# Stage orders of two attention layers, and logit indices loaded once: a four-layer graph network on one Trainium2 core

## The reference

```python
z = leaky_relu(xl[src] + xr[dst] + ee, 0.2)          # first and third attention layer
score = einsum('ehc,hc->eh', z, att)
m = segment_max(score, dst)
a = exp(score - m[dst])
denom = segment_sum(a, dst)
out = segment_sum(xl[src] * a / denom[dst], dst)
...
e = leaky_relu(h[src] @ a_src + h[dst] @ a_dst, 0.2)  # layer 2: edge logits
...
msg = all_msgs[edge_src, rel]                         # layer 3: 16 relation matrices
out = segment_sum(msg, edge_dst)
```

## Time and profile before

| | value |
|---|---|
| median of 3 runs | 7174.21 us |
| lowest, highest | 7170.84, 7176.18 us |
| profiled execution: its time | 7206.94 us |
| its span, first to last instruction | 7205.2 us |
| mean granted TensorE clock | 0.71 of full speed |
| DVE busy, share of the span | 75% |
| POOL busy, share of the span | 66% |
| PE busy, share of the span | 54% |
| ACT busy, share of the span | 44% |
| stage a, first to last gather start | 657.0 to 1724.7 us |
| stage g, first to last gather start | 5488.2 to 6528.8 us |
| logit stage, first to last gather start | 3456.2 to 3985.2 us |

### The profile page before, as it was taken

One profiled execution on the slowest core, in us unless ns is written; L12 is line 12 of the kernel. 1 busy time (PEld: TensorE's weight loads), 2 busy tenths in 40 slices (PEclk: granted clock), 3 DMA queues, 4 the chain that ended last, 5 costly groups with the idle time before them and its releaser, 6 DMA issues. The chain is left out here.

```text
span 7205.2 us, 84156 instructions
## 1 busy us (share of the span) xinstructions
PE 3879.4 (54%) x13024; PEld 2314.5 (32%) x13024; DVE 5386.3 (75%) x16939; ACT 3173.0 (44%) x7568; POOL 4760.7 (66%) x4609
## 2 busy tenths in 40 slices
PE   0001667664666665899000689868886766772000
PEld 0000233332333333788000345763332433441000
DVE  4502888886777777888676899767887888887886
ACT  0001666664333333777444100224554666665555
POOL 1777777775777776776677556016664777774776
PEclk9999776776788887555555789558997676665555
DMA  6001555555433343111799100569994555554554
GB/s 191 4 1 29 97 99 97 99 96 79 90 85 84 85 85 72 47 47 45 112 120 115 25 7 8 158 144 131 154 153 101 115 114 115 115 114 114 165 169 137
DMA packets 915728, 687.80 MB, mean 95 GB/s; under 512 B 604705, under 2 KB 754495, under 8 KB 914973
## 3 DMA queue, kind: packets, MB, share of 16 engines
q1 hardware_dynamic: 517456, 403.54, 21.1%
q0 software_dynamic: 147200, 139.08, 19.9%
q10 hardware_dynamic: 250888, 143.42, 6.6%
HBM read 491.36 MB, written 227.64 MB: 100 GB/s over the span
## 5 line engine op out<-in xcount | busy, mean ns | idle before, releaser
L802 POOL DMA_INDIRECT b_xg<-t_H,c_at x784 | 833.2, 1063 | 284.0 <-issue 238.4
L802 POOL DMA_INDIRECT g_xg<-t_D,c_at x784 | 803.4, 1025 | 320.1 <-issue 238.2
L802 POOL DMA_INDIRECT a_xg<-t_XL,c_at x784 | 830.6, 1059 | 250.3 <-issue 238.8
L1822 POOL DMA_INDIRECT f_dg<-t_D,c_at x392 | 377.0, 962 | 555.9 <-POOLq L179 358.7
L2210 POOL DMA_INDIRECT out<-n_yo,c_at x392 | 430.9, 1099 | 235.1 <-issue 116.1
L440 POOL DMA_INDIRECT t_XL<-su_pos,su_scatx x392 | 389.8, 994 | 245.6 <-DMA t_XL<-in_nodes 126.4
L1326 POOL DMA_INDIRECT l_d<-t_D,l_ix x392 | 397.7, 1014 | 183.8 <-issue 121.4
L1141 POOL DMA_INDIRECT t_RANK<-m_place,m_at x392 | 397.9, 1015 | 163.2 <-issue 116.4
L938 ACT ACTIVATE a_hn<-a_xg,a_sm 128x64 f32<-128x64 f32 x784 | 269.8, 430 | 401.0 <-DVE a_sm L675 400.1
L1375 ACT ACTIVATE l_hn<-l_xs,l_sm 128x64 f32<-128x64 f32 x784 | 265.0, 426 | 295.6 <-DVE l_sm L675 211.9
L2189 ACT ACTIVATE n_h<-n_x,n_sm 128x64 f32<-128x64 f32 (+1 forms) x800 | 269.4, 426 | 210.0 <-DVE n_sm L675 210.0
(11 more groups left out here) (455 smaller groups left out, 14037.6 us busy)
## 6 DMA issues: line engine op xcount, KB each, us to landing
a_ends<-t_LAST SPq DMA_DIRECT2D x98, 256.0 KB, 5.1
t_XSD<-a_xg SPq DMA_DIRECT2D x98, 256.0 KB
t_H<-a_oE ACTq DMA_DIRECT2D x98, 256.0 KB
b_ends<-t_LAST SPq DMA_DIRECT2D x98, 256.0 KB
l_xb<-t_XSD SPq DMA_DIRECT2D x49, 512.0 KB
f_rl<-t_REL SPq DMA_DIRECT2D x49, 512.0 KB
g_xb<-t_XSD SPq DMA_DIRECT2D x98, 256.0 KB
g_ends<-t_LAST SPq DMA_DIRECT2D x98, 256.0 KB, 5.2
```

The lines of the kernel that those rows point to most:

```text
L802: nc.gpsimd.indirect_dma_start(xg[k][:, j, i, :], None, table, bass.IndirectOffsetOnAxis(ap=C["at"][:, i, n * J + j:n * J + j + 1], axis=0 ...
L1822: nc.gpsimd.indirect_dma_start(dg[k][:, u, j, :], None, T["D2"], bass.IndirectOffsetOnAxis(ap=C["at"][:, 0, (2 * n + u) * J + j:(2 * n + u ...
```

## The change

Three edits. In stage a, DVE meets `denominator` first instead of behind `quotients`, and `quotients` go behind `sums`; ACT meets `normed` ahead of `features`; PE's `results` move from the end of the step to a place between `project` and `scores`, one step later (lag 5 instead of 4). In stage g, DVE's `norm` goes from the end of the step to its head with the same lag 1, ACT's `normed` gets lag 1 instead of 2, ACT's `results` lag 6 instead of 5, PE's `project` lag 2 instead of 3, `moments` lag 7 instead of 6, and PE's order in a step is new. In the logit stage the 49 index loads are replaced by one load of all indices into a tile `C["source"]` that outlives the blocks, issued by SP at the end of `mlp_block`; with them go SP's wait for landed gathers and POOL's wait for `ix`, and POOL's loop is written out in full. Stage b (wide) keeps its orders.

```diff
             if wide:
                 stages = [(L, leaky), (L + 2, quotients), (L + 1, denominator), (L + 1, sums), (L, maximum)]
+            elif tag == "a":
+                stages = [(4, denominator), (3, leaky), (4, sums), (5, quotients), (3, maximum), (1, norm)]
             else:
-                stages = [(L, leaky), (L + 2, quotients), (L + 1, sums), (L, maximum), (L - 2, norm)]
-                if not both:
-                    stages.insert(2, (L + 1, denominator))
+                stages = [(1, norm), (3, leaky), (5, quotients), (4, sums), (3, maximum)]
             flow(dve, stages, slots=SL)
...
+            elif tag == "a":
+                stages = [(3, values), (2, normed), (3, features), (2, turned), (3, exponents), (5, results)]
             else:
-                stages = [(L, values), (L, features), (L - 1, normed), (L - 1, turned), (L, exponents), (L + 2, results)]
+                stages = [(3, values), (3, features), (2, turned), (1, normed), (3, exponents), (6, results)]
             flow(act, stages, slots=SL, looped=tag != "a")
...
+            elif tag == "a":
+                stages = [(3, project), (5, results), (3, scores), (2, turn)]
             else:
-                stages = [(L, project), (L, scores), (L - 1, turn), (L + 1, results)]
-            if tag == "g":
-                stages.append((L + 3, moments))
+                stages = [(2, turn), (7, moments), (3, scores), (2, project), (4, results)]
             flow(pe, stages, slots=SL)
...
             flow(sp, [(0, load)], slots=SL)
+            sp.dma_start(C["source"][:, :].rearrange("p (n j) -> p n j", j=LOGIT_ROWS),
+                         T["PSRC"].rearrange("(n p j) -> p n j", p=P, j=LOGIT_ROWS)).then_inc(s_source, 16)
+            sp.wait_ge(s_source, 16)
...
                 if old:
-                    sp.wait_ge(s_g[k], NG * q)
-                sp.dma_start(ix[k][:, :], words_by(T["PSRC"], n, K)).then_inc(s_ix[k], 16)
-                if old:
-                    sp.wait_ge(s_xs, n - SL + 1)
+                    hold(sp, s_spturn, (s_xs, n - SL + 1))
...
             def gather(n, k, q, old):
-                hold(pool, s_turn, (s_ix[k], 16 * (q + 1)))
                 if old:
                     hold(pool, s_turn, (s_xs, n - SL + 1))
                 for j in range(K):
                     nc.gpsimd.indirect_dma_start(
                         d1[k][:, 0, j, :], None, T["D1"],
-                        bass.IndirectOffsetOnAxis(ap=ix[k][:, j:j + 1], axis=0)).then_inc(s_g[k], 16)
-            flow(pool, [(0, gather)], total=NB, slots=SL)
+                        bass.IndirectOffsetOnAxis(ap=C["source"][:, n * K + j:n * K + j + 1], axis=0)).then_inc(s_g[k], 16)
+            flow(pool, [(0, gather)], total=NB, slots=SL, looped=False)
```

More of the change, by code:

```diff
@@ L1121, in mlp_block @@
         s_at, s_rank, s_rturn, s_spturn = m.sems("at", SL), m.sems("rank", SL), m.sem("rturn"), m.sem("spturn")
+        s_source = m.sem("source")
         rank = T["RANK"].unsqueeze(1)
@@ L1278, in _ @@
                 act.wait_ge(s_st[k], 16 * chunks_of(k, SL))
+LOGIT_ROWS = 8
 def logit_block(nc, T, C):
@@ L1288, in logit_block @@
         SL = 4
-        K = 8
+        K = LOGIT_ROWS
         NB = EP // (P * K)
         slots = range(SL)
-        ix = [m.sb(f"ix{k}", [P, K], I32) for k in slots]
         d1 = [m.sb(f"d1{k}", [P, 2, K, D]) for k in slots]
@@ L1300, in logit_block @@
         sm = m.sb("sm", [P, 6, 2 * K])
-        s_ix, s_g, s_ld, s_hs, s_es = (m.sems(x, SL) for x in "ix g ld hs es".split())
-        s_xs, s_f, s_hn, s_e, s_ch, s_che, s_turn = (m.sem(x) for x in "xs f hn e ch che turn".split())
+        s_g, s_ld, s_hs, s_es = (m.sems(x, SL) for x in "g ld hs es".split())
+        s_xs, s_f, s_hn, s_e, s_ch, s_che, s_turn, s_spturn = (m.sem(x) for x in "xs f hn e ch che turn spturn".split())
         block = ctx.enter_context(nc.Block())
@@ L2267, in program @@
         C["at"] = m.sb("at", [P, 2, EF], I32)
+        C["source"] = m.sb("source", [P, EF], I32)
         prologue_block(nc, a, T, C)
```

## The result

The changed kernel takes 7089.07 us, median of 3 runs (7082.77 to 7089.41). Its ratio to the kernel before is 0.9871, 95% interval [0.9857, 0.9884], and 85 us less by the medians, whose own quotient is 0.9881.

A forecast was written before the change was run, and what follows sets the result against it. POOL's gathers, stretched by DVE scans on two SBUF tiles, were taken to bound stages a and g, DMA transfers the logit stage. Stage a -18, stage g 0, its end +8, logit -5 gave -15 us: median 7174.2 to 7159, range 7124 to 7189.

The forecast's parts named there:

- The bound: Stages a and g: POOL's gathers set the pace; their stretch, 88 and 61 us, is all a new order can win.
- phases are tied to landings while DVE waits, and DVE will wait in most steps: Stage a: reason for taking 18 us less, the stretch going from 0.90 to 0.72 us a step.
- a triangle's mean of 0.4: Stage a, rival of freely drifting scans: `den` stretches gathers 0.4 us a step on average, 49 us less; total 7128; chance 0.22.
- DVE's floor with 61 us: Stage a: largest gain allowed, if DVE's own work bounds the step at 10.3 us instead of 10.92: 61 us less.
- PE's and ACT's edits in stage a at nothing: Stage a: the moved PE and ACT work costs nothing, hidden by POOL's pace.
- I take 0: Stage g: no change in the gathers' stretch, since 58 of 98 steps already run without leaky's wait and the mean is 0.62.
- The ends (31 more, 61 less): Stage g: bounds around 0; 31 us more if each `num` catches a gather by 0.94, 61 less if none does.
- The end of stage g, +8: After stage g's last gathers: three rounds instead of two follow, a round taking 8.4 us, so 8 us more.
- The logit stage, -5: Logit stage: 5 us less, 3 for the start and 2 for the 49 little loads; ends 0 and -14.
- the 3 us of the start: Logit stage: the 3.05 us from SP's first issue to the first gather go almost whole, 3 us less.
- the 2 us of the little loads: Logit stage: dropping the 49 little loads gains 2 us of the 10.8 us that POOL waits for `ix` inside.
- the 18 us given to stage a: Stage a: stretch of 0.72 instead of 0.90 us a step over 98 steps, 18 us less; bounds 0 and 61 less.

The follow-up runs named there:

- before_msg_psum: Kernel before, all lists old, with stage a's product written to a PSUM bank as an operand of `num`: 7126.63 us, ratio 0.9945.
- after_more_dve: Changed kernel with a DVE memset of 290 columns (0.300 us) ahead of stage a's running maximum: 7108.23 us, ratio 0.9901 to the kernel before.
- a_only: Kernel before with the three new lists of stage a alone: 7112.99 us, ratio 0.9913.
- a_dve_only: Kernel before with DVE's new list of stage a alone, PE and ACT keeping their old orders there: 7123.87 us, ratio 0.992.
- g_moments_as_before: Changed kernel with stage g's `moments` last in PE's list again, at lag 6: 7086.73 us, ratio 0.9874 to the kernel before.
- g_shift: Kernel before with a DVE memset of 290 columns (about 0.3 us) ahead of stage g's product: 7149.39 us, ratio 0.9957.
- logit_only: Kernel before with the edit of the logit stage alone: 7160.7 us, ratio 0.9988.
- before_again: Kernel before with no edit, run once more for a second profiled execution: 7174.79 us, ratio 1.0004.
- b_msg_psum: Changed kernel with stage b's product written to the eighth PSUM bank: 7059.81 us, ratio 0.9841 to the kernel before.

## Why the prediction was wrong

**The bound, right.** POOL's gathers, stretched by DVE, were what could be won: the whole gain of stages a and g is in their busy time, and before_msg_psum shows the mechanism without any change of order. The Trainium skill, page "SBUF — State Buffer", section "Who interferes with whom", says that a VectorE instruction with two SBUF inputs contends with a GpSimd instruction that reads SBUF; the PSUM operand that freed the gathers agrees. What the section reports of a probe, that `tensor_tensor` did not stall the generation of descriptors, does not hold here: the product, a `tensor_tensor`, held the gather of 5691.50 by 0.35 us.

**Stage a: the step that failed is "phases are tied to landings while DVE waits, and DVE will wait in most steps".** Its first half was right: `num` goes off the gathers, `den` takes 0.72 where DVE waits, as in the early steps (10.7 us each). But it was worked out for a DVE that waits and then never asked whether the new pace leaves it anything to wait for. The same text had the floor, 10.2 to 10.5 us, beside a forecast step of 10.02 + 0.72 = 10.74; that looks like 0.3 us of room. But the room depends on the stretch. All ten waits for a landing lie in the first ten steps, the last six of them 0.31 to 0.41 us long. Then DVE halts 0.31 us (764.08) and 0.25 us (774.52) as its loop begins, `den` meets the next gather later and stretches it by 0.22 instead of 0.75, and POOL's step shrinks with it to 10.02 + 0.22 = 10.24, beside DVE's own 10.22: nothing is left to wait for.

From there DVE's pace, 10.29 with the loop's turns, is above POOL's undisturbed 10.02, and `den` slides to where it stretches the gathers by just the difference: 10.29 - 10.02 = 0.27 a step, measured 0.29. I took a triangle's mean of 0.4 for this case and called it a rival, with 0.22. The end named for it, DVE's floor with 61 us, is what came (55 to 59). That DVE is nearly the bound there now was tried (after_more_dve). What frees the phase was not tried and stays open. Six other traces with this DVE list, a_only and a_dve_only among them, show the same halts and a pace of 10.29 to 10.30; but in one of them, g_moments_as_before, DVE's last wait for a landing came at 687 us already, before any halt.

**PE's and ACT's edits in stage a at nothing: right** (a_dve_only).

**Stage g: the step that failed is "I take 0".** The reason for it, that 58 of 98 steps ran without leaky's wait already, took the time from the add to `num` as all that counts. That is not so: after the change that time is 5.96 and 6.47 us in two neighbouring steps. It also left out the product and the add, which held gathers for 10 and 12 us before. What changed is where the add itself begins, 0.3 to 0.5 us behind a gather's start, where before it was near it or 1.2 behind. `num`'s share of the stretch fell from 39 to 4 us, the whole from 58 to 23. The ends (31 more, 61 less) held the measured -35 to -38, but the middle was chosen by counting steps of the old pattern. g_shift shows that the scan's place against the gathers moves the time by itself; the moments' place and the late loads are excluded. Why the rows land at the other lag, 1.9 instead of 1.6 us behind the last gather's end, stays open: with the old lists one of seven profiled executions (logit_only) ran that way too.

**The end of stage g, +8: right**, 49.6 instead of 42.9 to 45.5, so 4 to 7.

**The logit stage, -5: the 3 us of the start measured 2.4; the 2 us of the little loads are 0** within what profiles tell. The 10.8 us of waits that this term was taken from were nearly all the first profile's own: inside the stage POOL waits for index loads 1.2 us in a_only and never in before_again.

**The sum.** -18 + 0 + 8 - 5 was forecast. Against before_again it is -55 in stage a, -35 in g, +4 at its end, -3 at the logit head: -89 by the stages. The spans of these two profiled executions differ by 77.5 us only, since in this pair the rest took some 10 us longer: stage b by 3, the logit stage by 2, the blocks between it and stage g by 7. The medians say 85, the ratio 92 us. So the direction and the cause came out as forecast, and the size did not: the 18 us given to stage a belong to a phase that lasted ten steps. (A slip beside it: half of the forecast's 0.40 was entered as 0.22.)

## What to carry to other kernels

Where an engine generates descriptors back to back, list which VectorE instructions read two SBUF tiles and where each begins against the next gather; one operand moved to a free PSUM bank can free the gathers without any change of order, but then book the stretch anew, since other instructions move against the gathers too (27 us at leaky in b_msg_psum). A phase worked out for an engine that waits holds only as long as it waits: compare its own work per step with the new pace, for once it is above the other engine's undisturbed pace, the stretch becomes just the difference of the two. And change the lists of a software pipeline together or show that one suffices: PE's list alone cost 303 us where the set gained 35 in its stage, while in stage a DVE's list alone did it all.

## What the hardware showed that was not expected

- A gather that a scan catches late is stretched little: begun 0.87 ahead of it, 0.22 (1403.62); begun 0.33 ahead, 0.75 (731.79). In both the gather ends 0.75 or 0.76 us after the scan.
- A scan with one operand in PSUM takes the same 1.28 us for 512 columns as one with two in SBUF, and holds nothing.
- A memset alone holds nothing, but with a product right behind it the pair does. In after_more_dve 53 gathers began under the memset, with no two-input instruction behind it, and took 0.94 or 0.95 us. In g_shift 29 did, and all ended 0.80 to 0.83 us after the product, though in 26 of them the product began behind the gather, by up to 0.22 us; the gather of 6005.78 is one. Why a product begun behind a gather holds it there, and in no other run, is open. Two lines of after_more_dve:

```profile
1106.57 0.30 DVE L855 MEMSET a_spare<- 128x290 f32 x1
1106.65 0.94 POOL L803 DMA_INDIRECT a_xg<-t_XL,c_at  x1 [0.30 <-issue]
```

- Executions of the same lists may differ by 30 us in one stage alone (stage g with the old lists: 1008 in logit_only, 1036 to 1047 in six others), so a single pair of profiles can't price an edit of that size.
